# Naturals at three quarters of the prior unit, row stores and bias additions later, warm-up transposes, gate and up in one stage

## The chip, the cores and the metric

The kernel runs on one core of one Trainium2 chip. The metric is device time in microseconds (us) of one execution, as the median of a few runs. A profile is one more execution, taken by the hardware profiler. TensorE is called PE, VectorE DVE, ScalarE ACT, GpSimd POOL, and SP (SyncE) only issues DMAs.

## What is computed

x is (2, 1024, 256) in float32, 2048 rows of 256. Its layer norm xn feeds a causal attention with 16 heads of 16 and a mixture of 8 experts with the two best per row; both are added to x.

```
xn = layernorm(x)
q, k, v = xn @ Wq + bq, xn @ Wk + bk, xn @ Wv + bv        # 16 heads of 16
attn = softmax(q @ k.T * 0.25 + causal) @ v, heads joined, @ Wo + bo
logits = xn @ Wr; the two largest, softmax over the two
moe = sum over the two: p * ((clip(silu(xn @ Wg[e]), -7, 7) * (xn @ Wu[e])) @ Wd[e])
out = x + attn + moe
```

## The kernel before

**Shapes and tiles.** The 2048 rows are 16 tiles of 128. Heads are taken four at a time, so attention is 8 units (UNITS: two batches by four groups). A unit has 12 steps (STEPS), each of one block of 128 keys against up to 512 queries, for four heads. In a step the scores are transposed (keys on partitions), the exponential is taken by ACT from PSUM (`exps`, line 838), POOL masks the diagonal blocks (`mask`, line 776), and PE weighs v (`weigh_v`, line 1232) into one bank per 512 queries.

**Naturals and negated maxima.** The exponential needs the row maximum first. So each unit's scores are also computed the natural way round (`natural`, line 1194, queries on partitions, 48 chunks a unit), DVE takes the maximum of each (`row_max`, lines 939 and 942), negates them and splits them into three bfloat16 parts (lines 956 to 959), PE transposes them (line 1200), DVE copies them to negt (line 966), and SP copies negt by DMA into three extra rows of packq (`neg_rows`, line 665). The first scores of the unit (`scores`, line 1213) wait for that copy. The naturals of unit u run beside the scores of unit u - 1.

**q and k.** PE projects them (`qk_product`, line 1125), ACT takes the high part in bfloat16 (line 810), DVE the residual (line 911), ACT the middle part (line 816), POOL the low part (line 738). SP stores all parts to DRAM (line 642) and loads them packed by head for each unit (`load`, line 655: three runs, each for q and for k, for each half: twelve DMAs a unit). There are three slots (SLOTS), so the loads of unit u wait for the last scores of unit u - 3.

**Start.** SP loads x in four parts, DVE takes mean and variance and writes xn (line 902) into the memory that probs uses later, PE transposes it (`transpose_xn`, line 1118), ACT copies it, and ACT's queue stores xn to DRAM (`store_xn`, line 795) for the gathers. The first exponential and the first gather wait for these stores. v and the router's logits come from line 1149.

**Experts.** After routing (DVE, lines 1004 to 1090, and PE lines 1157 to 1175) 39 tiles of 128 rows are worked on: POOL gathers rows (line 752) and fetches the expert's weights (line 762, 3 slots) by indirect DMA, PE transposes the rows (line 1265), does gate and up as two stages `gu1` and `gu2` into one bank (line 1272), ACT takes tanh (line 866), DVE makes the hidden values (lines 1097, 1100), PE multiplies down (line 1293), ACT scales (line 872), POOL scatters the rows to DRAM (line 768). POOL also adds the output bias to x, tile by tile (`add_bias_to_x`, line 744); the attention projection (line 1258) is added to that later (line 998), and SP reads the expert rows back and DVE adds them (lines 987, 989).

**Order.** At build time a planner (`Planner`, `make_plan`) lists all stages as jobs with an engine, a cost in ns, what they come after, a due time, a lag until the result is seen, the PSUM bank they take or free, and a size for large DMAs (bytes over 65536 count at 280 per ns on one common line). It goes through them greedily: for each engine the job that can start first, ties by due time (on PE, 8000 is added to the due of a kind other than the one before), and of the engines the earliest. The result is a fixed list per engine and the bank of each result; each engine then walks its list (`walk`) and waits on semaphores. The planner's numbers only set the order; they are not waits. Attention is due from 40000 to 415000 ns, the experts from 85000 to 375000. These lines set what the change touches:

```
return begin + (end - begin) * 0.9 * sum(nat_weight[:m]) / sum(nat_weight)      # nat_due, line 260
job("ACT", ("ln", q), 420, [("DVE", ("ln", q))], due=2000 + q, lag=2000, size=524288)      # row stores, line 271
job("POOL", ("residual", t), 700, [("DVE", ("bias",)), ("DVE", ("ln", 3))], 110000 + 8000 * t)      # line 319
```

## Time and profile before

| | us |
|---|---|
| runs, median of 3 | 490.92 |
| runs, lowest and highest | 488.54, 501.08 |
| profiled execution, its own time | 493.95 |
| its span in the profile | 492.1 |

Start times are microseconds from the start of the span; the span is shorter than the execution's own time by what lies around it. A row of the timeline or of a group names the engine (PEld is PE's weight load, SPq the queue that SP issues into), the line, the operation, out<-in and the count; in brackets stands how long the engine was idle before it and what ended that. PEclk is the granted TensorE clock as a share of full speed. In this profile a matmul of float32 is recorded as two.

### The profile page before, as it was taken

Reading aid. Unit: us, or ns where it says so; the run is one execution under the profiler, and the core shown is the slowest. Engines: PE = TensorE matmul, PEld = TensorE weight load, DVE = VectorE, ACT = ScalarE, POOL = GpSimd, SP = SyncE. Lnnn points to the kernel's source line nnn. Section 1 sums busy time; section 2 is a strip of 40 time slices with the busy share of each in tenths; the row PEclk is TensorE's granted clock in tenths of the full one; section 3 lists DMA queues with packets and bytes.
Section 4 is the critical chain, followed back from the end, with each engine's and each line's share of the span. In section 5 each row is a group of like instructions: output and inputs, shape, how many; then the busy total and the mean of one; then the engine's idle time right before and its main releaser. Section 6 shows DMA issues by size and latency. Waiting matters only on the chain.

```text
span 492.1 us, 8376 instructions
## 1 busy us (share of the span) xinstructions
PE 433.8 (88%) x2791; PEld 255.0 (52%) x2791; DVE 323.1 (66%) x1007; ACT 245.0 (50%) x607; POOL 200.3 (41%) x239
## 2 busy tenths in 40 slices
PE   0995973968997999899979999799979999999996
PEld 0673531553234456465655666456646565566443
DVE  4824899669786577656646558456665675766394
ACT  0561562231564564565436444565465545664972
POOL 4320289553025126343535246334454365433211
PEclk9997996887898999899989999999999999999999
DMA  8379861481009226943594229624394454340491
GB/s 269 133 215 160 170 143 65 142 285 44 1 20 224 113 77 194 185 133 117 188 199 159 85 98 230 148 84 168 113 252 130 153 161 128 128 156 15 151 313 52
DMA packets 40374, 71.35 MB, mean 145 GB/s; under 512 B 5893, under 2 KB 30598, under 8 KB 40332
## 3 DMA queue, kind: packets, MB, share of 16 engines
q0 software_dynamic: 9360, 39.99, 25.5%
q1 hardware_dynamic: 27996, 27.54, 24.2%
q10 hardware_dynamic: 2976, 3.29, 2.1%
q8 instruction: 23, 0.38, 0.3%
q14 instruction: 19, 0.16, 0.1%
HBM read 55.85 MB, written 15.60 MB: 145 GB/s over the span
## 4 chain that ended last, share of the span: by engine, by line
PE 48%; issue 23%; DVE 9%; DMA 8%; ACT 5%; POOL 4%; SPq 3%; POOLq 0%; ACTq 0%; DVEq 0%
PE psum L1232 9%; PE psum L1213 9%; PE psum L1272 9%; PE psum L1194 9%; PE psum L1293 5%; ACT probs L838 3%; DMA packq<-negt 3%; SPq L655 2%; DVE psum L939 2%; PE psum L1125 2%; DMA x<-in_x 2%; DMA packk<-qk_parts 2%; PE psum L1258 2%; POOL probs L776 1%; DMA xg<-xn_rows,token 1%
## 5 line engine op out<-in xcount | busy, mean ns | idle before, releaser
L838 ACT ACTIVATE probs<-psum 128x512 f32<-128x512 f32 (+3 forms) x384 | 159.4, 507 | 74.7 <-PE psum L1213 65.4
L939 DVE CUSTOM_DVE_ANT_0 psum<-psum,maskrow 128x128 f32<-128x128 f32 (+3 forms) x256 | 122.2, 504 | 45.2 <-PE psum L1194 44.6
L1213 PE MATMUL psum<-packq,packk 99*128 99x512 bf16 (+3 forms) x384 | 99.7, 343 | 16.3 <-DMA packq<-negt 11.3
L1194 PE MATMUL psum<-packk,packq 96*128 96x512 bf16 (+3 forms) x384 | 100.8, 344 | 7.8 <-DMA packk<-qk_parts 5.5
L942 DVE TENSOR_REDUCE mxa<-psum 128x1 f32<-128x512 f32 x128 | 87.8, 686 | 20.1 <-PE psum L1194 19.8
L1232 PE MATMUL psum<-probs,v 128*32 128x512 f32 (+3 forms) x768 | 79.1, 505 | 9.6 <-POOL probs L776 8.7
L1272 PE MATMUL psum<-xgt,wexp 128*128 128x128 f32 x624 | 84.6, 282 | 0.2 <-ACT xgt L859 0.2
L1272 PEld LDWEIGHTS psum<-xgt,wexp 128*128 128x128 f32 x624 | 80.2, 197 | 8.5 <-issue 6.0
L776 POOL TENSOR_SCALAR_AFFINE_SELECT probs<-probs 128x512 f32<-128x512 f32 x64 | 43.9, 689 | 96.8 <-ACT probs L838 96.2
L762 POOL DMA_INDIRECT wexp<-in_wexp,wrow x39 | 37.5, 960 | 93.8 <-PE psum L1293 87.0
L1213 PEld LDWEIGHTS psum<-packq,packk 99*128 99x128 bf16 x384 | 34.9, 99 | 70.8 <-issue 21.7
L1194 PEld LDWEIGHTS psum<-packk,packq 96*128 96x128 bf16 x384 | 36.7, 100 | 51.4 <-issue 12.5
L752 POOL DMA_INDIRECT xg<-xn_rows,token x39 | 37.8, 968 | 26.8 <-PE psum L1265 20.1
L768 POOL DMA_INDIRECT expert_rows<-yo,slots x39 | 39.9, 1023 | 17.0 <-issue 11.1
L1293 PE MATMUL psum<-wexp,hid 128*128 128x256 f32 x156 | 42.6, 396 | 0.5 <-ACT probs L838 0.3
L1097 DVE SCALAR_TENSOR_TENSOR tanh<-tanh,psum 128x256 f32<-128x256 f32 x39 | 16.3, 418 | 35.2 <-ACT tanh L866 31.4
L1232 PEld LDWEIGHTS psum<-probs,v 128*32 128x32 f32 x768 | 18.1, 110 | 36.2 <-issue 26.5
L1293 PEld LDWEIGHTS psum<-wexp,hid 128*128 128x128 f32 x156 | 26.8, 191 | 18.5 <-issue 11.1
L872 ACT ACTIVATE yo<-psum 128x256 f32<-128x256 f32 x39 | 15.0, 385 | 42.5 <-PE psum L1293 42.0
L738 POOL TENSOR_TENSOR stage<-resid,stage 128x512 bf16<-128x512 f32 x16 | 19.8, 1246 | 36.9 <-ACT stage L816 36.8
L1125 PE MATMUL psum<-xnt,wqk 128*128 128x512 f32 x64 | 33.3, 634 | 1.0 <-DVE prod L1037 1.0
L866 ACT ACTIVATE tanh<-psum 128x256 f32<-128x256 f32 x39 | 15.1, 388 | 31.3 <-PE psum L1272 30.7
(114 smaller groups left out, 385.9 us busy)
## 6 DMA issues: line engine op xcount, KB each, us to landing
qk_parts<-stage SPq DMA_DIRECT2D x24, 256.0 KB, 3.2
stage<-expert_rows SPq DMA_DIRECT2D x16, 256.0 KB, 4.3
packq<-qk_parts SPq DMA_DIRECT2D x16, 192.0 KB, 5.4
packk<-qk_parts SPq DMA_DIRECT2D x16, 192.0 KB, 5.7
x<-in_x SPq DMA_DIRECT2D x4, 512.0 KB, 9.2
xn_rows<-probs ACTq DMA_DIRECT2D x4, 512.0 KB, 3.2
packq<-qk_parts SPq DMA_DIRECT2D x16, 128.0 KB, 6.1
packk<-qk_parts SPq DMA_DIRECT2D x16, 128.0 KB, 5.9
```

Of the source, the lines that this page charges most:

```text
L752: pool.indirect_dma_start(out=xg[:, i % 2, :], out_offset=None, in_=xn_d, in_offset=bass.IndirectOffsetOnAxis(ap=token[:, i:i + 1], axis=0))\
L768: pool.indirect_dma_start(out=z_d, out_offset=bass.IndirectOffsetOnAxis(ap=slots[:, i:i + 1], axis=0), in_=yo[:, i % 2, :], in_offset=None ...
L776: pool.affine_select(out=cols, in_=cols, compare_op=ALU.is_ge, fill=0.0, base=0, pattern=[[0, UH], [1, P]], channel_multiplier=-1).then_in ...
L838: act.activation(probs[:, g % RING, h, 0:width], psum[:, bank, 0:width], ACT.Exp, scale=SCALE)\
L939: ins = dve.tensor_tensor_reduce(out=chunk, in0=chunk, in1=maskrow[:, BANK - width:], scale=1.0, scalar=NEG, op0=ALU.add, op1=ALU.max, acc ...
L942: ins = dve.tensor_reduce(into, chunk, op=ALU.max, axis=AX.X)
L1125: return pe.matmul(psum[:, bank, :], wqk[:, op, c, P * grp:P * (grp + 1)], xnt_moe[:, c, cols], start=c == 0, stop=c == DC - 1)
L1194: pe.matmul(psum[:, bank, 0:width], packq[0:MAXROW, u % SLOTS, i // HALF, h, P * (i % HALF):P * (i % HALF + 1)], packk[0:MAXROW, u % SLOTS ...
L1213: pe.matmul(psum[:, bank, 0:width], packk[0:KROWS, u % SLOTS, j // HALF, h, P * (j % HALF):P * (j % HALF + 1)], packq[0:KROWS, u % SLOTS, ...
L1232: ins = pe.matmul(psum[32 * h:32 * h + 32, bank, t0 - BANK * c:BANK], v[:, TB * b + j, at:at + 32], probs[:, g % RING, h, 0:width], start= ...
L1272: ins = pe.matmul(psum[:, bank, P * m:P * (m + 1)], wexp[:, i % WSLOTS, at:at + P], xgt[:, i % 2, c, :], start=c == 0, stop=c == DC - 1)
L1293: ins = pe.matmul(psum[:, bank, 0:D], hid[:, i % 2, P * c:P * (c + 1)], wexp[:, i % WSLOTS, at:at + D], start=c == 0, stop=c == DC - 1)
```

## The change

- `nat_due`: the naturals of a unit are due over the first 0.75 (SPREAD) of the prior unit and not 0.9.
- The lag of the copy of the negated maxima (`("SP", ("neg", x))`) is 8000 (NEG_LAG) and not 2200.
- The row stores of xn (`("ACT", ("ln", q))`) are due at 34000 and not 2000, and come after the first load of unit 0.
- The bias addition of tile t (`("POOL", ("residual", t))`) comes after scatter t in POOL's list.
- The loads of unit 1 are due at 60000 and not 20000; the loads of unit 0 have a lag of 4500 and not 2500.
- Gather, fetch and scatter cost 1250, 1300 and 1300 and not 1000; a gather counts with 131072 bytes and has a lag of 2200.
- `gu1` and `gu2` become one stage `gu` of 1850, in `gate_up`: the same products in the same order, with nothing between them.
- Before its list PE does 60 (WARM) transposes of the identity into bank 7, as soon as the first constants are there.

No wait on a semaphore is added or taken away other than the one in `warm_clock`; the lists of all engines are planned anew.

```diff
--- before.py
+++ after.py
@@ -234,8 +234,11 @@
 SWITCH = {("b", "b"): 5, ("f", "f"): 15, ("b", "f"): 95, ("f", "b"): 20, ("b", "c"): 105, ("f", "c"): 105,
           ("c", "b"): 110, ("c", "f"): 120}
 STAY = 8000
+NEG_LAG = 8000
+SPREAD = 0.75
 RATE = 280
 SMALL = 65536
+WARM = 60
 PACE = dict(attention=(40000, 415000), experts=(85000, 375000))
 
 
@@ -257,7 +260,7 @@
         if u == 0:
             return 5000 if m < EARLY else 30000 + 400 * (m - EARLY)
         begin, end = due_at[NS * (u - 1)], due_at[NS * u]
-        return begin + (end - begin) * 0.9 * sum(nat_weight[:m]) / sum(nat_weight)
+        return begin + (end - begin) * SPREAD * sum(nat_weight[:m]) / sum(nat_weight)
 
     for n, (ns, due) in enumerate(((1100, -30), (2000, 30), (1800, 31))):
         job("POOL", ("const", n), ns, due=due)
@@ -268,7 +271,7 @@
         job("DVE", ("stats", q), 1900, [("SP", ("x", q))], due=10 * q)
         job("POOL", ("rstd", q), 960, [("DVE", ("stats", q))], due=-20)
         job("DVE", ("ln", q), 1280, [("POOL", ("rstd", q))], due=10 * q - 5)
-        job("ACT", ("ln", q), 420, [("DVE", ("ln", q))], due=2000 + q, lag=2000, size=524288)
+        job("ACT", ("ln", q), 420, [("DVE", ("ln", q)), ("SP", ("load", 0, 0, 0))], due=34000 + q, lag=2000, size=524288)
         for c in range(DC):
             pe(("xnt", q, c), 436, [("DVE", ("ln", q))], due=10 * q, takes=("xnt", q, c))
             job("ACT", ("xnt", q, c), 478, [("PE", ("xnt", q, c))], due=10 * q, frees=("xnt", q, c))
@@ -316,7 +319,7 @@
     pe(("bias",), 853, [("DVE", ("widen",))], 30000, takes=("bias",))
     dve(("bias",), 425, [("PE", ("bias",))], 30000, frees=("bias",))
     for t in range(NT):
-        job("POOL", ("residual", t), 700, [("DVE", ("bias",)), ("DVE", ("ln", 3))], 110000 + 8000 * t)
+        job("POOL", ("residual", t), 700, [("DVE", ("bias",)), ("DVE", ("ln", 3)), ("POOL", ("scatter", t))], 110000 + 8000 * t)
 
     for u in range(UNITS):
         b, g = divmod(u, G)
@@ -324,9 +327,9 @@
             after = [("SP", ("store", 4 * b + 2 * (g // 2) + c))]
             if u >= SLOTS:
                 after += [("PE", ("s", NS * (u - SLOTS + 1) - 1, UH - 1))]
-            due = 8 + 10 * c if u == 0 else 20000 + c if u == 1 else nat_due(u, 0) - 30000 + c
+            due = 8 + 10 * c if u == 0 else 60000 + c if u == 1 else nat_due(u, 0) - 30000 + c
             for r in range(len(RUNS)):
-                job("SP", ("load", u, c, r), 900, after, due, lag=2500, size=131072)
+                job("SP", ("load", u, c, r), 900, after, due, lag=2500 if u else 4500, size=131072)
 
     for u in range(UNITS):
         for m in range(NCH):
@@ -340,7 +343,7 @@
         dve(("negate", x), 1200, [("DVE", ("max", u, m))], due)
         pe(("neg", x), 60, [("DVE", ("negate", x))], due, ("neg", x), "b")
         dve(("neg", x), 220, [("PE", ("neg", x))], due, ("neg", x))
-        job("SP", ("neg", x), 550 if c1 - c0 == 2 else 1600, [("DVE", ("neg", x))], 0, lag=2200, size=8192)
+        job("SP", ("neg", x), 550 if c1 - c0 == 2 else 1600, [("DVE", ("neg", x))], 0, lag=NEG_LAG, size=8192)
 
     for g in range(NS * UNITS):
         u, n = divmod(g, NS)
@@ -387,20 +390,19 @@
         after = [("DVE", ("list",)), ("ACT", ("ln", 3))] if i == 0 else []
         if i >= 2:
             after += [("PE", ("x", i - 2))]
-        job("POOL", ("gather", i), 1000, after, due - 8000, lag=2000)
+        job("POOL", ("gather", i), 1250, after, due - 8000, lag=2200, size=131072)
         after = [("DVE", ("experts",)), ("PE", ("list",))] + ([("PE", ("d", i - WSLOTS))] if i >= WSLOTS else [])
-        job("POOL", ("fetch", i), 1000, after, due - 9000, lag=2000, size=128 * WROW * 4)
+        job("POOL", ("fetch", i), 1300, after, due - 9000, lag=2000, size=128 * WROW * 4)
         pe(("x", i), 220, [("POOL", ("gather", i))], due, ("x", i))
-        job("ACT", ("xgt", i), 252, [("PE", ("x", i))] + ([("PE", ("gu2", i - 2))] if i >= 2 else []), due,
+        job("ACT", ("xgt", i), 252, [("PE", ("x", i))] + ([("PE", ("gu", i - 2))] if i >= 2 else []), due,
             frees=("x", i))
-        pe(("gu1", i), 875, [("ACT", ("xgt", i)), ("POOL", ("fetch", i))], due + 500, ("gu", i))
-        pe(("gu2", i), 875, [("PE", ("gu1", i))], due + 500)
-        job("ACT", ("tanh", i), 280, [("PE", ("gu2", i))] + ([("DVE", ("hid", i - 2))] if i >= 2 else []), due + 1000)
+        pe(("gu", i), 1850, [("ACT", ("xgt", i)), ("POOL", ("fetch", i))], due + 500, ("gu", i))
+        job("ACT", ("tanh", i), 280, [("PE", ("gu", i))] + ([("DVE", ("hid", i - 2))] if i >= 2 else []), due + 1000)
         dve(("hid", i), 780, [("ACT", ("tanh", i))] + ([("PE", ("d", i - 2))] if i >= 2 else []), due + 1000, ("gu", i))
         pe(("d", i), 853, [("DVE", ("hid", i))], due + 2000, ("d", i))
         job("ACT", ("yo", i), 280, [("PE", ("d", i))] + ([("POOL", ("scatter", i - 2))] if i >= 2 else []), due + 2000,
             frees=("d", i))
-        job("POOL", ("scatter", i), 1000, [("ACT", ("yo", i))], due + 2000, lag=1800)
+        job("POOL", ("scatter", i), 1300, [("ACT", ("yo", i))], due + 2000, lag=1800)
 
     for t in range(NT):
         after = [("POOL", ("scatter", MAX_TILES - 1)), ("SP", ("store", QKS // 2 - 1)), ("DVE", ("gates",))]
@@ -415,7 +417,7 @@
 
 
 ORDER, BANK_OF, PLANNED = make_plan()
-FIRST_OF = {"qk1": "qk", "gu1": "gu"}
+FIRST_OF = {"qk1": "qk"}
 
 
 def fill_of(stage):
@@ -1109,6 +1111,11 @@
 
         @block.tensor
         def _(pe):
+            def warm_clock():
+                pe.wait_ge(consts, 1)
+                for _ in range(WARM):
+                    pe.transpose(psum[:, BANKS - 1, 0:P], ident[:, :], ident[:, :])
+
             def transpose_xn(q, c):
                 if q == 0 and c == 0:
                     pe.wait_ge(consts, 1)
@@ -1265,25 +1272,16 @@
                     ins = pe.transpose(psum[:, bank, P * c:P * (c + 1)], xg[:, i % 2, P * c:P * (c + 1)], ident[:, :])
                 ins.then_inc(full, 1)
 
-            def gu_product(i, m):
-                bank, _ = FILL_AT[("gu", i)]
-                for c in range(DC):
-                    at = 2 * F * c + P * m
-                    ins = pe.matmul(psum[:, bank, P * m:P * (m + 1)], wexp[:, i % WSLOTS, at:at + P], xgt[:, i % 2, c, :],
-                                    start=c == 0, stop=c == DC - 1)
-                return ins
-
-            def gate_up_first(i):
+            def gate_up(i):
                 pe.wait_ge(fetch_in[i % WSLOTS], 16 * (i // WSLOTS + 1))
                 wait_freed(pe, ("x", i))
-                wait_room(pe, ("gu", i))
-                for m in range(F // P):
-                    gu_product(i, m)
-
-            def gate_up(i):
-                for m in range(F // P, 2 * F // P):
-                    ins = gu_product(i, m)
-                ins.then_inc(filled[FILL_AT[("gu", i)][0]], 1)
+                bank, full = wait_room(pe, ("gu", i))
+                for m in range(2 * F // P):
+                    for c in range(DC):
+                        at = 2 * F * c + P * m
+                        ins = pe.matmul(psum[:, bank, P * m:P * (m + 1)], wexp[:, i % WSLOTS, at:at + P], xgt[:, i % 2, c, :],
+                                        start=c == 0, stop=c == DC - 1)
+                ins.then_inc(full, 1)
 
             def down(i):
                 wait_freed(pe, ("gu", i))
@@ -1294,10 +1292,11 @@
                                     start=c == 0, stop=c == DC - 1)
                 ins.then_inc(full, 1)
 
+            warm_clock()
             walk("PE", {"xnt": transpose_xn, "qk1": project_qk_first, "qk2": project_qk, "v": project_v, "route": route,
                         "list": list_tokens, "bias": project_bias, "nat": natural, "neg": transpose_neg, "s": scores,
                         "pv": weigh_v, "y_t": transpose_y, "proj_t": transpose_heads, "proj": project, "x": transpose_rows,
-                        "gu1": gate_up_first, "gu2": gate_up, "d": down})
+                        "gu": gate_up, "d": down})
 
 
 _SHAPES = {
```

## Rows read from the trace of the kernel before

**Rows 1.** The page, part 1: busy time, share of the span, instructions

```profile
PE 433.8 (88%) x2791; PEld 255.0 (52%) x2791; DVE 323.1 (66%) x1007; ACT 245.0 (50%) x607; POOL 200.3 (41%) x239
```

**Rows 2.** Windows by stage; the first row names the columns

```profile
core 0: us, PE busy (x) PEld busy (x) DVE busy (x) ACT busy (x) POOL busy (x), PEclk, DMA share, GB/s
...
42.35:64.00 21.65, 21.65 (x104) 13.03 (x105) 17.61 (x99) 8.53 (x22) 5.19 (x5) 0.92 0.94 167
64.00:86.00 22.00, 11.68 (x57) 3.61 (x56) 21.48 (x30) 9.12 (x22) 19.76 (x21) 0.79 0.38 96
86.00:148.00 62.00, 54.77 (x285) 25.90 (x284) 49.41 (x159) 22.92 (x50) 20.39 (x22) 0.85 0.30 99
148.00:460.00 312.00, 295.60 (x2080) 182.50 (x2079) 195.62 (x619) 169.82 (x428) 135.71 (x156) 0.98 0.51 143
```

**Rows 3.** What PE waited for: total us, times, longest us

```profile
PE psum L1213 <- DMA packq<-negt: 11.3, 5, 3.2
PE psum L1232 <- POOL probs L776: 8.7, 8, 5.1
...
PE psum L1213 <- issue: 2.6, 2, 1.9
```

**Rows 4.** Timeline at the starts of two units: start us, us, what

```profile
243.67 0.30 SPq L655 DMA_DIRECT2D packq<-qk_parts  x1
...
246.41 0.73 SPq L665 DMA_DIRECT2D packq<-negt  x1
...
253.69 1.43 PE L1213 MATMUL psum<-packq,packk 99*128 99x512 bf16 x4 [3.21 <-DMA packq<-negt]
...
452.23 0.71 SPq L665 DMA_DIRECT2D packq<-negt  x1
...
455.32 1.04 PE L1213 MATMUL psum<-packq,packk 99*128 99x512 bf16 x4 [0.66 <-DMA packq<-negt]
```

**Rows 5.** Windows, a stretch after a hole

```profile
156.00:160.00 4.00, 4.00 (x16) 1.58 (x15) 3.03 (x12) 3.60 (x11) 1.31 (x3) 0.50 1.08 255
```

**Rows 6.** The page, part 5: groups by line

```profile
L939 DVE CUSTOM_DVE_ANT_0 psum<-psum,maskrow 128x128 f32<-128x128 f32 (+3 forms) x256 | 122.2, 504 | 45.2 <-PE psum L1194 44.6
...
L942 DVE TENSOR_REDUCE mxa<-psum 128x1 f32<-128x512 f32 x128 | 87.8, 686 | 20.1 <-PE psum L1194 19.8
...
L1272 PEld LDWEIGHTS psum<-xgt,wexp 128*128 128x128 f32 x624 | 80.2, 197 | 8.5 <-issue 6.0
...
L768 POOL DMA_INDIRECT expert_rows<-yo,slots x39 | 39.9, 1023 | 17.0 <-issue 11.1
```

**Rows 7.** Timeline, PE at the start

```profile
12.82 3.65 PE L1118 MATMUL psum<-ident,probs 128*128 128x128 f32 x16 [12.82 <-DVE probs L902]
...
16.26 4.81 PE L1125 MATMUL psum<-xnt,wqk 128*128 128x512 f32 x8
...
21.79 3.60 PE L1125 MATMUL psum<-xnt,wqk 128*128 128x512 f32 x8
...
25.23 1.91 PE L1118 MATMUL psum<-ident,probs 128*128 128x128 f32 x16
```

**Rows 8.** Timeline, up to the first natural

```profile
26.00 1.27 ACT L810 ACTIVATE stage<-psum,bqk 128x512 bf16<-128x512 f32 x2 [2.48 <-DVE probs L902]
...
32.10 0.48 SPq L655 DMA_DIRECT2D packq<-qk_parts  x1
...
42.35 0.82 PE L1194 MATMUL psum<-packk,packq 96*128 96x128 bf16 x3 [5.48 <-DMA packk<-qk_parts]
```

**Rows 9.** Bias additions by their line; the timeline of a mask

```profile
L744 POOL TENSOR_TENSOR x<-x,bo x16: 717/730/1286, 62.3 to 85.4; 128x256 f32<-128x256 f32 x16
...
76.49 2.69 POOL L776 TENSOR_SCALAR_AFFINE_SELECT probs<-probs 128x512 f32<-128x512 f32 x1
...
79.32 1.51 PE L1232 MATMUL psum<-probs,v 128*32 128x384 f32 x8 [5.07 <-POOL probs L776]
```

**Rows 10.** Timeline, the transposes of the second gather

```profile
103.05 0.44 PE L1265 MATMUL psum<-ident,xg 128*128 128x128 f32 x2 [3.85 <-DMA xg<-xn_rows,token]
```

## The prediction

> **What bounds the kernel now.** I read the busy times of the engines first. PE is busy 433.8 of 492.1 us, DVE 323.1, ACT 245.0, POOL 200.3 [rows 1]. So PE bounds it, and the time can fall in two ways: PE stands still for less than its 58.3 us, or its busy time shrinks because less of it runs at the lower of the clock's two levels (1.2 instead of 2.4 GHz). The windows by stage [rows 2] say where both lie. Standing still (length less busy): 10.3 us at 64 to 86, 7.2 at 86 to 148, 16.4 at 148 to 460. Lost to the clock ((1 - PEclk) x busy): 1.7 us at 42 to 64, 2.5 at 64 to 86, 8.2 at 86 to 148, 5.9 at 148 to 460. Then the list of what PE waited for: the copy of the negated maxima into packq 11.3 us, masked probability tiles 8.7, "issue" ahead of a score 2.6 [rows 3]; and single rows for 12.82 us before the first transpose [rows 7], 5.48 before the first natural [rows 8], 3.85 for a gather [rows 10]. The change aims at all of these but the 12.82.
>
> Every engine walks a fixed list that the planner wrote. At each step it takes the job that can start soonest, and a due time decides only among jobs that can start at the same instant. So a later due does not hold a job back on an idle engine; a dependency, a longer lag or a longer cost does.
>
> **The naturals and the lag of the negated maxima.** Take the stretch around 250. The loads that an old unit's end sets free begin at 243.67; the copy of the maxima is issued at 246.41, six loads ahead of it and six behind; PE stands from 250.48 to 253.69 [rows 4]. That is 7.3 us from issue to use. The copy at 452.23, with no loads beside it, had its scores at 455.32, 3.1 us later, with 0.66 us of standing [rows 4]. The plan reckoned 2.2 us. With SPREAD 0.75 the naturals end earlier by 0.15 of a unit's pace of (415 - 40) / 8 = 46.9 us, that is 7.0 us; so the copy would go out near 239.4, ahead of the loads, and land near 242.5. With NEG_LAG 8 us the plan puts other stages between besides. What can go is 11.3 + 2.6 = 13.9 us [rows 3]. The loads themselves remain, with fetches and gathers beside them, so some wait returns under another name. I take -10 (from -13.9 to -3).
>
> After such a hole PE comes back at the low level: at 156 to 160 the granted clock is 0.50 with PE busy for all 4 us [rows 5]. The 5.9 us of clock at 148 to 460 are of this kind: -4.5 (-5.9 to 0).
>
> The price is a denser DVE. From 148 to 460 it is busy 195.6 of 312 us, 63% [rows 2]. Its maxima take (87.8 + 122.2) / 323.1 = 65% of its busy time [rows 1, 6], so 0.41 of the time. In the stretch where naturals lie that makes 0.41 / 0.9 + 0.22 = 68% now and 0.41 / 0.75 + 0.22 = 77% then. It has room, but on PE a natural whose bank isn't free stops everything behind it. One reduction takes 0.686 us [rows 6]; half a one waited for in every third of the 7 x 12 steps that have naturals beside them is 9.6 us, none is 0. No wait for maxima is among PE's large ones now, so I take a third: +3 (0 to +10).
>
> **The start.** PE begins at 12.82. Its first 16 transposes take 3.65 us against 1.91 for 16 later ones, and its first 8 records of L1125 4.81 against 3.60 [rows 7]. So it starts at the low level: the 8 records are 1.21 us too long, which is 2.4 us at half pace, so the rise came near 18.7. Sixty transposes from the ready identity on (near 1.9) run at 3.44 / 16 = 0.215 us each, start to start, at the low level and 0.119 at the high one. If the clock rises 4 to 5.6 us in, they are through near 11, in time that is idle anyway, and the two groups run 1.7 + 1.2 = 2.9 us shorter. If it never rises, they end at 14.8, 2.0 us late.
> The row stores move behind the first load in ACT's list. The fourth now waits for the last rows, and the high parts of the next two tiles stand behind it: they start at 26.00, after 2.48 us of ACT idle [rows 8]. They can go some 1.5 us earlier; residual, middle and low part, store and first load (32.10) follow. Against this, 2 MB of row stores now flow beside the loads, which need from 32.10 to 42.35 as it is [rows 8]. At the 255 GB/s of window 156 to 160 [rows 5], 2 MB are 8.2 us of all queues; between none and half of it falls ahead of the first natural, I take 1. The later due of unit 1's loads does nothing: SP is idle and takes them at once. So -2.9 - 1.5 + 1, about -3.5 (-6 to +3). The first exp comes after 64, so the stores have time to land.
> On the clock a page speaks against the sixty transposes. What this trace shows: the rise near 18.7 came 5.9 us after the first transpose but 2.4 us after the first product of L1125 [rows 7]; from 42.35 on, with PE busy throughout, a mean of 0.92 over 21.65 us is 3.5 us at the low level [rows 2]. The Trainium skill ("TensorE: Matmul & The Clock Gate", Part 4) says that transposes do not count as busy for the clock. By that rule the warm-up costs the 2.0 us and the sum is 4.9 us higher; this trace leans the other way, products alone having needed 3.5 us and not 2.4.
>
> **Bias additions.** Their due of 110 us did nothing: all 16 lie between 62.3 and 85.4, 0.73 us in the median and up to 1.29 [rows 9], among the masks. The mask of 76.49 took 2.69 us, and PE stood 5.07 us for it [rows 9]. Tied to scatters, which come far behind the routing, they leave POOL free and this mask starts up to 2 us sooner; how long it takes beside the DVE stays open. 8.7 us of mask waits are there in all [rows 3]; they bound it. But until 86 the DVE's routing (busy 21.48 of 22 us [rows 2]) decides what follows. PE's product of the token list stands behind the waits, so experts can begin earlier. -3 (-8.7 to 0). The 16 x 0.73 us come back among gathers, on a POOL that is 43% busy.
>
> **Costs of gather, fetch, scatter.** A scatter measured 1.02 us with 11.1 / 39 = 0.28 of issue ahead of it [rows 6]; the plan had 1.0 and gets 1.3. PE stood 3.85 us for the second gather at 103.05 [rows 10]; now the plan counts its bytes and can put naturals there. -2 (-4 to +2). With an earlier start and fewer holes up to 148, some of the 12.4 us of clock before 148 returns, but there the DVE sets the pace: -2 (-6 to +2).
>
> **Gate and up in one stage.** No product goes. The weight loads of L1272 have 8.5 us of idle before them, 6.0 by "issue" [rows 6], mostly where another kind stood between the halves. I take a quarter; and a score may now wait up to half a stage more: -1.5 (-3 to +1).
>
> **Sum.** -10 - 4.5 + 3 - 3.5 - 3 - 2 - 2 - 1.5 = -23.5 on the profiled execution's own 493.95 us (span 492.1 and 1.85 around it): 470.5. The median of the runs shown is 490.92, 0.6% less; 470.5 x 490.92 / 493.95 = 467.6, so 468.
>
> **Rivals.**
> (1) *The hole is the load burst, not the maxima.* If full queues hold up fetches, gathers and instructions as well, the row of the maxima vanishes and its time returns under other names: the -14.5 shrink to -3, 482 on the profile, 479. For it: 2.6 us go by "issue", with no engine named [rows 3], and DMA share is 1.08 beside the low clock [rows 5]. Against: PE's row names the copy, and the copy free of loads cost 0.66 us.
> (2) *The start gives nothing.* The clock does not rise and the row stores delay the first load: +2 in place of -3.5 gives 476, so 473. For it the loads' 10 us as they are; against, the dated rise.
> (3) *The early stretch gives more.* The token list and the experts move up by the whole wait, and half of the 12.4 us of clock comes back: 9 us more, 461.5, so 459. Against: the DVE's 21.48 of 22 us.
> (4) *Slower: the DVE becomes the bound.* Naturals pressed into three quarters make PE wait a whole reduction, 0.686 us, at each step. Without the +3 the gains are 26.5 us; 39 such waits undo them and 53 make it slower by 2%. There are 84 steps; at 60 it is 41 us: 508.6, so 505. For it: PE's fixed order; against: 77%.
>
> **How the numbers follow.** Forecast 0.60, (1) 0.15, (2) 0.13, (3) 0.08, (4) 0.04. The forecast's own terms, taken as independent, give about 11 us to each side. The range reaches below (3) and above (1): 455 to 484. Two per cent, about what a measurement of this kernel can tell from no change, is 481. Below it lie the forecast, (2), (3) and over half of (1), less tails: 0.84 faster, 0.12 within, 0.04 slower.
>
> **What would show it.** Right: under 3 us of waits for the copy; SP issues the copy ahead of a unit's loads; the first records of L1125 at 0.45 us each; no bias addition before 120; first natural near 39; PE idle under 9 us at 148 to 460; granted clock over 0.97. Wrong: a new wait for wexp or xg of 10 us; scores or naturals waiting over 10 us for maxima; PE busy, warm-up left out, not under 428.

## The result and the profile after

The changed kernel takes 464.67 us in the median of four runs (459.69 to 469.68), the kernel before 492.27 (488.54 to 501.08): a ratio of 0.939 (0.926 to 0.953). All ratios of this document are taken from the fast executions of each kernel alone, so they are not the quotients of the medians beside them. A second series gave 474.01 against 498.82, 0.955 (0.949 to 0.961). Forecast were 468 us and a range of 455 to 484. The profiled execution is the slowest of its four, 469.68 us with a mean granted clock of 0.960; the fastest, 459.69, had 0.985, and the fastest of the second series, 471.72, had 0.967.

Page of the changed kernel, part 1, against [rows 1]:

```profile
PE 436.3 (93%) x2851; PEld 261.7 (56%) x2851; DVE 317.2 (68%) x1007; ACT 242.3 (52%) x607; POOL 197.9 (42%) x239
```

Sixty more PE instructions and 24.2 us less of span (467.9 for 492.1). The windows say where, against [rows 2] (PE stands for a window's length less its busy time):

```profile
core 0: us, PE busy (x) PEld busy (x) DVE busy (x) ACT busy (x) POOL busy (x), PEclk, DMA share, GB/s
0.00:86.00 86.00, 73.78 (x374) 44.39 (x375) 62.46 (x212) 35.70 (x88) 33.92 (x48) 0.94 0.68 187
86.00:148.00 62.00, 54.06 (x301) 31.92 (x301) 51.47 (x172) 22.63 (x53) 21.32 (x24) 0.86 0.41 125
148.00:440.00 292.00, 286.76 (x2046) 173.25 (x2047) 187.85 (x589) 170.63 (x434) 139.94 (x164) 0.99 0.52 148
440.00:468.00 28.00, 21.67 (x133) 12.15 (x130) 15.41 (x36) 13.32 (x34) 2.71 (x4) 0.94 0.48 155
```

The same windows of the kernel before:

```profile
0.00:86.00 86.00, 57.38 (x251) 33.47 (x252) 58.01 (x188) 33.26 (x83) 39.48 (x56) 0.91 0.70 165
...
148.00:440.00 292.00, 276.46 (x1934) 170.46 (x1933) 184.30 (x585) 156.66 (x393) 128.34 (x146) 0.98 0.54 150
```

PE stands still for 5.2 us at 148 to 440 where it had stood for 15.5. Up to 86 it stands for 12.2 instead of 28.6, but 8.1 of these 16.4 us are filled by the warm-up. From 86 to 148 it stands 7.9, against 7.2 [rows 2]. So the standing time falls by 26.7 us in all (58.3 to 31.6); the warm-up takes 8.1 back, and the busy time without it falls by 5.6 (433.8 to 428.2): 26.7 - 8.1 + 5.6 = 24.2.

What PE waited for, against [rows 3]:

```profile
engine line waited for: us in total, times, longest us
PE psum L1282 <- DMA wexp<-in_wexp,wrow: 5.6, 2, 3.9
PE psum L1125 <- DVE probs L904: 2.7, 2, 2.4
PE psum L1201 <- DVE prod L1039: 2.4, 1, 2.4
...
PE psum L1239 <- POOL probs L778: 1.8, 4, 0.7
```

The copy of the maxima (11.3 us before) has no row left, the masks fell from 8.7 to 1.8. At the start of a unit the copy now leaves ahead of all twelve loads, here by 4.8 us, and the scores that need it (231.20, 8.6 us after its issue) run without a wait, where [rows 4] had six loads ahead of it and 3.21 us of standing:

```profile
222.63 0.73 SPq L667 DMA_DIRECT2D packq<-negt  x1
227.40 0.31 SPq L657 DMA_DIRECT2D packq<-qk_parts  x1
...
231.20 1.03 PE L1220 MATMUL psum<-packq,packk 99*128 99x512 bf16 x4
```

One large hole beside a burst is left, in another unit: weights are fetched at 145.20, at the end of twelve loads issued from 138.81 to 145.27, and PE waits for them until 150.06. (The other 1.8 us of this row, at 117.12, have no loads beside them.)

```profile
145.20 0.98 POOL L764 DMA_INDIRECT wexp<-in_wexp,wrow  x1 [0.30 <-PE psum L1272]
...
150.06 3.78 PE L1282 MATMUL psum<-xgt,wexp 128*128 128x128 f32 x16 [3.85 <-DMA wexp<-in_wexp,wrow]
```

After it the 16 products take 3.78 us, against 2.0 for such a stage elsewhere (101.10), and the granted clock of 150 to 154 is 0.50: the low level behind a hole is seen again.

The start, against [rows 7, 8]:

```profile
2.01 8.14 PE L1117 MATMUL psum<-ident 128*128 128x128 f32 x60 [2.01 <-POOLq L729]
...
12.57 1.07 PE L1125 MATMUL psum<-ident,probs 128*128 128x128 f32 x8 [2.43 <-DVE probs L904]
...
14.87 3.60 PE L1132 MATMUL psum<-xnt,wqk 128*128 128x512 f32 x8
...
28.67 0.49 SPq L657 DMA_DIRECT2D packq<-qk_parts  x1
...
36.74 0.76 PE L1201 MATMUL psum<-packk,packq 96*128 96x128 bf16 x5
```

The 60 transposes are through at 10.15. The next eight take 1.07 us, 0.134 each, in spite of 2.43 us of idle between; the first records of the q and k product take 3.60, not 4.81. The first load comes 3.4 us earlier, the first natural 5.6. The row stores went out at 35 to 37 as meant. The bias additions moved too (62.3 to 85.4 before [rows 9]), though not behind 120 as the prediction had it:

```profile
L746 POOL TENSOR_TENSOR x<-x,bo x16: 723/740/771, 104.2 to 255.0; 128x256 f32<-128x256 f32 x16
```

Yet a faster start shows little at the end, as the runs below say.

### The profile page after: what moved, and what is told of

Its sections match the earlier page's. It is cut to its first block, busy times and chain, and to the rows that moved or that the text cites. A ratio compares the mean times of both kernels' runs of the same rounds, so it can differ in the third digit from the quotient of the medians.

```text
span 467.9 us, 8496 instructions
## 1 busy us (share of the span) xinstructions
PE 436.3 (93%) x2851; PEld 261.7 (56%) x2851; DVE 317.2 (68%) x1007; ACT 242.3 (52%) x607; POOL 197.9 (42%) x239
## 4 chain that ended last, share of the span: by engine, by line
PE 72%; DMA 12%; DVE 5%; ACT 4%; issue 3%; POOL 2%; SPq 1%; ACTq 0%; POOLq 0%
PE psum L1282 15%; PE psum L1239 14%; PE psum L1220 13%; PE psum L1201 11%; PE psum L1291 7%; DMA xg<-xn_rows,token 4%; PE psum L1265 3%; DMA qk_parts<-stage 3%; DMA wexp<-in_wexp,wrow 3%; ACT probs L840 3%; PE psum L1132 2%; PE psum L1156 2%; DMA x<-in_x 2%; PE psum L1272 2%; PE psum L1247 1%
## 5 line engine op out<-in xcount | busy, mean ns | idle before, releaser
L840 ACT ACTIVATE probs<-psum 128x512 f32<-128x512 f32 (+3 forms) x384 | 156.1, 515 | 39.4 <-PE psum L1220 38.8
L944 DVE TENSOR_REDUCE mxa<-psum 128x1 f32<-128x512 f32 x128 | 88.0, 687 | 28.7 <-PE psum L1201 28.7
L1201 PE MATMUL psum<-packk,packq 96*128 96x512 bf16 (+3 forms) x384 | 97.5, 333 | 3.8 <-DVE prod L1039 2.4
L1220 PE MATMUL psum<-packq,packk 99*128 99x512 bf16 (+3 forms) x384 | 98.0, 335 | 2.8 <-DVE mxa L944 1.2
L1239 PE MATMUL psum<-probs,v 128*32 128x512 f32 (+3 forms) x768 | 78.0, 507 | 2.8 <-POOL probs L778 1.8
L770 POOL DMA_INDIRECT expert_rows<-yo,slots x39 | 39.6, 1015 | 23.2 <-ACT yo L874 12.3
L874 ACT ACTIVATE yo<-psum 128x256 f32<-128x256 f32 x39 | 15.0, 385 | 42.3 <-PE psum L1291 36.7
L740 POOL TENSOR_TENSOR stage<-resid,stage 128x512 bf16<-128x512 f32 x16 | 18.4, 1164 | 32.5 <-ACT stage L818 32.5
L1132 PE MATMUL psum<-xnt,wqk 128*128 128x512 f32 x64 | 30.7, 600 | 0.8 <-DVE resid L913 0.8
```

What stands on the lines that cost most here:

```text
L770: pool.indirect_dma_start(out=z_d, out_offset=bass.IndirectOffsetOnAxis(ap=slots[:, i:i + 1], axis=0), in_=yo[:, i % 2, :], in_offset=None ...
L840: act.activation(probs[:, g % RING, h, 0:width], psum[:, bank, 0:width], ACT.Exp, scale=SCALE)\
L944: ins = dve.tensor_reduce(into, chunk, op=ALU.max, axis=AX.X)
L1132: return pe.matmul(psum[:, bank, :], wqk[:, op, c, P * grp:P * (grp + 1)], xnt_moe[:, c, cols], start=c == 0, stop=c == DC - 1)
L1201: pe.matmul(psum[:, bank, 0:width], packq[0:MAXROW, u % SLOTS, i // HALF, h, P * (i % HALF):P * (i % HALF + 1)], packk[0:MAXROW, u % SLOTS ...
L1220: pe.matmul(psum[:, bank, 0:width], packk[0:KROWS, u % SLOTS, j // HALF, h, P * (j % HALF):P * (j % HALF + 1)], packq[0:KROWS, u % SLOTS, ...
```

## The experiments

Three series, each on one chip with runs of the kernel before beside it; ratios are to that. The first has the changed kernel again, no warm-up, the row stores early and the naturals back; the second the copy first, the two constants alone, the long lag without the early naturals and the bias additions free; the third all others. Only the first has the changed kernel in it. That kernel came out at 0.939 (the result above) and 0.955, so a ratio of one series is compared with one of another to no better than 1.6%, some 8 us.

### The changed kernel again, and three of its parts undone

The changed kernel:

> The changed kernel itself, for comparison on the same chip. Ratio to the kernel before 0.94 (0.93 to 0.95). If its runs differ by over 1% among themselves again, the differences should follow the granted clock (0.96 to 0.985 so far), not the waits.

474.01 us, 0.955 (0.949 to 0.961).

Without the warm-up:

```diff
-WARM = 60
+WARM = 0
```

> The changed kernel with WARM 0; all lists stay as they are. Theory A, the start is on the path: the first 16 transposes and the first 8 records of L1132 run at the low level, 2.9 us more, first natural at 39 to 40 instead of 36.7, the whole 3 us slower than the changed kernel. Theory B, the DVE's routing swallows it: first natural as late, but the token list's product at about the same time (76) and the whole within 1 us. Theory C, transposes do not count for the clock: nothing changes in the first groups.

472.67 us, 0.949 (0.941 to 0.956): no slower. The first natural is at 38.6 instead of 36.7, but the token list at 74.9 against 75.4. Its first transposes:

```profile
12.96 3.38 PE L1125 MATMUL psum<-ident,probs 128*128 128x128 f32 x16 [12.96 <-DVE probs L904]
16.18 3.60 PE L1132 MATMUL psum<-xnt,wqk 128*128 128x512 f32 x8
```

Here the q and k product begins 1.3 us later than in the changed kernel and runs at the high level from its first record. So the clock came up during 16 transposes, with only idle time before them. In the kernel before the same 16 had not brought it up by their end, and the product behind them took 4.81 us [rows 7]; of the four kernels traced here without a warm-up two rose by the end of the 16 and two behind it. The Trainium skill ("TensorE: Matmul & The Clock Gate", Part 4) says that a transpose does not count as busy for the clock in the way of other products. These two rows, and the 1.07 us behind the sixty, speak against that for float32 transposes as this kernel does them.

The row stores ahead of the first load again:

```diff
-        job("ACT", ("ln", q), 420, [("DVE", ("ln", q)), ("SP", ("load", 0, 0, 0))], due=34000 + q, lag=2000, size=524288)
+        job("ACT", ("ln", q), 420, [("DVE", ("ln", q))], due=2000 + q, lag=2000, size=524288)
```

> The changed kernel with the row stores due at 2000 and without their dependency, as before; only ACT's list changes. Theory A, the fourth store's wait holds up the high parts: first load 1.5 to 2 us later than 28.67 and the whole 1 to 2 us slower. Theory B, stores beside loads cost more than the wait: first load later, but the loads land faster, so that the first natural comes no later than 36.7 and the whole is the same or up to 1 us faster.

473.45 us, 0.952 (0.947 to 0.957). The first load goes out at 30.9, not 28.7, and the first natural at 38.7, not 36.7; the end does not move. Not all of the 2 us are the stores': in this trace PE was idle for 2.03 us behind the 60 transposes, the granted clock was 0.50 from 13 to 16, the 16 transposes of xn took 3.49 us, and the first product began at 16.10, not 14.87. So the warm-up did not hold the level in this execution.

The naturals and the lag as before, the rest of the change kept:

```diff
-NEG_LAG = 8000
-SPREAD = 0.75
+NEG_LAG = 2200
+SPREAD = 0.9
```

> The changed kernel with SPREAD 0.9 and NEG_LAG 2200. Theory A, the copy of the maxima makes the holes: its waits come back (over 8 us in the list of PE's waits), with 4 us of clock, and the whole is 12 to 15 us slower than the changed kernel, ratio to before 0.965 to 0.97. Theory B, the load burst makes them: the row of the copy comes back, the waits for wexp (5.6 us) go, the whole is 3 to 5 us slower, ratio 0.945 to 0.95.

485.73 us, 0.976 (0.969 to 0.982), 11.7 us above the changed kernel on the same chip. What PE waited for:

```profile
PE psum L1220 <- DMA packq<-negt: 15.5, 6, 4.0
```

The wait is back, longer than in the kernel before. The two constants are worth 11.7 us here, and all the rest of the change together 13.1 (498.82 to 485.73).

### Is it the copy's place in the queue?

The two constants do two things: they move naturals, and they change the plan's order on SP, where every copy now stands ahead of later units' loads. The kernel before had two, one, three and five of the plan's loads (each is two DMAs) of later units ahead of the copies of units 1 to 4. The next kernel is the kernel before with that order alone changed, everything else as planned:

```diff
+for _x in range(2, len(NEGS)):
+    _sp = ORDER["SP"]
+    _at = _from = _sp.index(("neg", _x))
+    while _sp[_from - 1][0] == "load" and _sp[_from - 1][1] > _x:
+        _from -= 1
+    _sp[_from:_at + 1] = [_sp[_at], *_sp[_from:_at]]
```

> The kernel before; only SP's list changes: each copy of the negated maxima from unit 1 on goes ahead of the loads of later units that stood just before it. All other lists stay. Theory A, the copy waits for the loads issued ahead of it: it lands about 3 us after issue instead of 7, PE's waits for it fall from 11.3 to under 4 us, and with some clock the whole is 6 to 10 us faster than before, ratio 0.98 to 0.985. Theory B, the loads behind it hold it up as much as those ahead of it: waits stay over 8 us, ratio 0.995 to 1.0. Theory C, the burst moves on to other waits: the copy's row falls, others for wexp or xg rise by as much, ratio 0.995 to 1.0.

481.93 us against 492.88, 0.974 (0.968 to 0.981). Its windows and its wait at the same unit start as in [rows 4]:

```profile
148.00:440.00 292.00, 284.72 (x1998) 177.13 (x1996) 190.16 (x605) 162.47 (x407) 131.30 (x150) 0.98 0.55 154
```

```profile
236.85 0.73 SPq L671 DMA_DIRECT2D packq<-negt  x1
237.69 0.39 SPq L661 DMA_DIRECT2D packq<-qk_parts  x1
...
243.69 1.89 PE L1219 MATMUL psum<-packq,packk 99*128 99x512 bf16 x4 [2.43 <-DMA packq<-negt]
```

Standing time at 148 to 440 falls from 15.5 to 7.3 us, and the waits for the copy from 11.3 to 5.9. The copy goes out 9.6 us earlier, yet with twelve loads right behind it still takes 6.8 us from issue to use (7.3 in [rows 4], 3.1 with no loads near). The kernel before had one copy ahead of its burst too, and PE waited 2.71 us for it:

```profile
354.92 0.73 SPq L665 DMA_DIRECT2D packq<-negt  x1
...
361.62 1.04 PE L1213 MATMUL psum<-packq,packk 99*128 99x512 bf16 x4 [2.71 <-DMA packq<-negt]
```

There it is 5.3 us with two load DMAs ahead (194.31 to 199.62), 7.3 with six, 9.9 with ten (302.96 to 312.84), and 6.7 with none. So for most copies the place in the queue buys an earlier issue more than a quicker landing; being first does not give the 3.1 us. Whether it is the loads behind it that slow it was not separated: a fetch of expert weights (768 KB) goes out up to 1 us before the copies at 236.85 and 354.92 too, and none beside the one that took 3.1. Moving 22 load DMAs behind four copies is worth some 11 us with no instruction more or less.

The two constants alone, on the kernel before:

```diff
-        job("SP", ("neg", x), 550 if c1 - c0 == 2 else 1600, [("DVE", ("neg", x))], 0, lag=2200, size=8192)
+        job("SP", ("neg", x), 550 if c1 - c0 == 2 else 1600, [("DVE", ("neg", x))], 0, lag=NEG_LAG, size=8192)
```

(and 0.75 for 0.9 in `nat_due`, NEG_LAG = 8000)

> The kernel before with SPREAD 0.75 and NEG_LAG 8000 alone. Theory A, this part is worth 11.5 us by itself (-10 of waits, -4.5 of clock, +3 of denser DVE): ratio 0.975 to 0.98. Theory B, the parts need each other: the first 150 us stay as they are, and the later gain is under 5 us, ratio over 0.99. The copy's row goes to under 1 us in either.

489.87 us, 0.997 (0.993 to 1.001). The plan has every copy ahead of later units' loads here as well. No wait for the copy is left in its list; others are there:

```profile
PE psum L1234 <- POOL probs L778: 11.3, 10, 5.1
PE psum L1196 <- ACT yo L874: 5.3, 1, 5.3
```

The span is 488.8, the standing time 54.5 us against 58.3. It lies elsewhere now: a natural waits 5.28 us at 157.87 for a bank that ACT's `yo` was to free, masks cost 2.6 us more, and the end after 440 has 9.5 us of standing instead of 6.9. So the copy wait can be removed and nothing gained, if the new plan has holes of its own.

The long lag kept, the naturals at 0.9 again, in the changed kernel:

```diff
-SPREAD = 0.75
+SPREAD = 0.9
```

> The changed kernel with SPREAD 0.9 and NEG_LAG 8000 kept. Theory A, the lag alone makes the plan put other stages before the scores: waits for the copy stay under 3 us although it goes out beside the loads, and the whole is within 4 us of the changed kernel. Theory B, the early issue is what counts: waits for the copy over 5 us, 8 us slower or more.

482.59 us, 0.979 (0.974 to 0.984). Its list of waits, and one unit start:

```profile
PE psum L1272 <- DMA xg<-xn_rows,token: 14.1, 4, 5.9
PE psum L1282 <- DMA wexp<-in_wexp,wrow: 4.6, 2, 3.0
```

```profile
227.94 0.73 SPq L667 DMA_DIRECT2D packq<-negt  x1
...
229.50 0.95 POOL L754 DMA_INDIRECT xg<-xn_rows,token  x1 [0.30 <-issue]
...
238.63 0.69 PE L1272 MATMUL psum<-ident,xg 128*128 128x128 f32 x2 [5.85 <-DMA xg<-xn_rows,token]
```

The copy is issued behind eight of the twelve loads again. The plan allows it 8 us and puts expert work in the gap; but that work's gather was issued in the same burst, and PE waits for it until 238.63, 9.1 us after its issue. Of the copy a wait of 1.9 us is left in all. This is rival (1), the hole under another name; in this kernel it holds as long as the copy stays in the burst.

Last, both constants undone in the changed kernel (as in the 485.73 us kernel above), with the copies moved ahead by the six lines:

> The changed kernel with SPREAD 0.9 and NEG_LAG 2200 (which cost 2.1% of the time before, 0.9756 against 0.9551), but with each copy of the maxima put ahead of the loads of later units in SP's list. Theory A, the order on SP's queue is all that the naturals part brings: ratio 0.95 to 0.96, PE's waits for the copy fall from 15.5 us to under 6. Theory B, the copy's head start of some 7 us is needed too: waits for it stay at 6 to 9 us and the ratio at 0.96 to 0.97.

468.79 us against 501.06, 0.943 (0.937 to 0.948).

```profile
PE psum L1226 <- DMA packq<-negt: 3.8, 2, 3.2
```

The order alone brings back what the constants brought, within what two series can tell: with naturals at 0.9 and a lag of 2.2 us, 0.976 without the order becomes 0.943 with it. Two kernels of the same series that keep the constants, with one other part undone each, took 463.80 and 464.39 us, so up to 5 us may be theirs.

### The bias additions

```diff
-        job("POOL", ("residual", t), 700, [("DVE", ("bias",)), ("DVE", ("ln", 3)), ("POOL", ("scatter", t))], 110000 + 8000 * t)
+        job("POOL", ("residual", t), 700, [("DVE", ("bias",)), ("DVE", ("ln", 3))], 110000 + 8000 * t)
```

> The changed kernel with the bias additions free to start on an idle POOL, as before; POOL's list changes, PE's in a twelfth of its places. Theory A, they hold up masks and so the token list: its product comes 3 to 5 us later than 75.9, and the whole is 3 us slower than the changed kernel. Theory B, DVE alone sets the early stretch: the product stays within 1 us of 75.9 and the whole within 1 us.

468.40 us against 492.88, 0.952 (0.947 to 0.957). They run at 57.2 to 79.0 again, and the token list comes at 79.9 instead of 75.4. Whether these 4 us reach the end stays open: 0.952 lies between the changed kernel's 0.955 and 0.939 of two other series, and a loss of 3 us is less than that can show.

### The plan's costs, the lag of the loads, and the halves of gate and up

Costs of gather, fetch and scatter at 1000, the gather with a lag of 2000 and without its bytes:

> The changed kernel with gather, fetch and scatter at 1000 and a gather without bytes. Theory A, the real costs keep PE from meeting gathers and scatters before they land: waits for xg, wexp and what stands behind scatters rise from 6 us to over 12, whole 5 to 8 us slower. Theory B, they matter little: within 2 us.

464.39 us against 501.06, 0.934 (0.928 to 0.941).

```profile
86.00:148.00 62.00, 58.85 (x374) 36.82 (x374) 54.49 (x184) 26.44 (x64) 32.37 (x37) 0.94 0.61 179
```

PE stands 3.2 us in this stretch instead of 7.9, at a clock of 0.94 instead of 0.86. The truer costs bought nothing there.

The lag of unit 0's loads at 2500:

> The changed kernel with unit 0's loads at a lag of 2500 again. Theory A, the longer lag lets the v products be done while the loads fly, so that routing starts early: without it DVE's first routing instruction comes 3 us or more later than 46.9, the token list's product at 79 or later, and PE is idle for 5 us more at 64 to 88; whole 3 to 5 us slower. Theory B, the early stretch has no path to the end: the product comes later, the whole stays within 2 us, as with the bias additions.

463.80 us, 0.932 (0.927 to 0.937): no loss either. Both are at or a little below the changed kernel's 0.939 and 0.955; as they were not timed beside it, that either is faster stays open.

Gate and up as two stages again, with the functions for them as in the kernel before:

```diff
-        pe(("gu", i), 1850, [("ACT", ("xgt", i)), ("POOL", ("fetch", i))], due + 500, ("gu", i))
+        pe(("gu1", i), 875, [("ACT", ("xgt", i)), ("POOL", ("fetch", i))], due + 500, ("gu", i))
+        pe(("gu2", i), 875, [("PE", ("gu1", i))], due + 500)
```

> The changed kernel with gate and up as two stages again. Forecast of the prediction: 1.5 us slower. Rival from the busy times: PE's busy time less its clock loss is 415.2 us before and 415.0 after without the warm-up, so the merged stage saved nothing and the whole stays within 1 us.

484.21 us against 501.06, 0.971 (0.963 to 0.979). In the same series the three kernels with one stage, each with another part undone, took 463.80, 464.39 and 468.79: 15 to 20 us less. Against the changed kernel, in other series, it is 0.971 / 0.955 to 0.971 / 0.939, 1.7 to 3.4%: 8 to 16 us. Its windows:

```profile
86.00:148.00 62.00, 53.13 (x271) 25.76 (x271) 50.23 (x170) 20.00 (x48) 17.80 (x21) 0.82 0.41 117
148.00:440.00 292.00, 282.10 (x1963) 174.77 (x1962) 183.96 (x582) 159.93 (x404) 136.93 (x160) 0.98 0.49 142
440.00:486.00 46.00, 36.46 (x251) 20.20 (x249) 21.46 (x50) 26.08 (x69) 8.76 (x12) 0.96 0.42 138
```

Up to 86 it does the same as the changed kernel. By 440 it has 251 matmuls left where the other has 133. Of the 18.2 us between the two profiled spans (486.1 and 467.9) 8.2 are standing time and 10.0 more busy time, about 5 of these by the clock ((1 - PEclk) x busy is 21 us in all against 16). The first expert tile shows how this starts. With one stage, in the changed kernel:

```profile
87.60 3.75 PE L1282 MATMUL psum<-xgt,wexp 128*128 128x128 f32 x16 [1.27 <-issue]
...
95.06 0.42 DVE L1099 SCALAR_TENSOR_TENSOR tanh<-tanh,psum 128x256 f32<-128x256 f32 x1
...
98.01 1.08 PE L1291 MATMUL psum<-wexp,hid 128*128 128x256 f32 x4
```

With two:

```profile
88.14 1.66 PE L1280 MATMUL psum<-xgt,wexp 128*128 128x128 f32 x8 [0.51 <-issue]
...
90.14 2.00 PE L1280 MATMUL psum<-xgt,wexp 128*128 128x128 f32 x8
...
134.52 1.99 PE L1301 MATMUL psum<-wexp,hid 128*128 128x256 f32 x8
```

With two stages the down product of the first tile comes at 134.52 (147.57 in the kernel before), and the first scatter at 137.2 (150.2). With one it comes at 98.01, the scatter at 100.6. Up to 148 there are 80 records of gate and up products and 20 of down products in the changed kernel, 56 and 12 with two stages. The halves are no slower themselves, 1.05 to 1.13 us each at the high level against 2.0 for both. What comes after them is late. DVE's first hidden values, with two stages:

```profile
113.76 0.41 DVE L1100 SCALAR_TENSOR_TENSOR tanh<-tanh,psum 128x256 f32<-128x256 f32 x1
114.20 0.42 DVE L1103 SCALAR_TENSOR_TENSOR hid<-tanh,psum 128x256 f32<-128x256 f32 x1
```

ACT's tanh for them was done at 92.6, so they stood 21 us in DVE's list, and another 20 in PE's until 134.52. In the changed kernel the same step begins at 95.06, 3.3 us after its tanh. Why the plan puts them so late when the stage is halved was not settled. In every kernel run here with one stage the first scatter lies at 97 to 103, in every one with two at 137 to 151. That halving the stage costs the time is shown; that it costs it by the late down products is read from these rows and was not tested by itself.

## Why the prediction was right, and where it was not

The total, 468 against 464.67, is nearer than the steps deserve.

**Naturals, copy and clock behind the holes.** Forecast -10 and -4.5, with +3 against them: -11.5. Undoing the two constants costs 11.7 us; doing only what they do to SP's order gains 11 on the kernel before. The mechanism was the one named: the copy went out behind the loads. That it takes naturals ending 7.0 us earlier to put it right was half of it: the order does it without them. And that the two constants are worth this by themselves was wrong: on the kernel before, with the order they bring and no wait for the copy left, they gave 0.997. Nor does a copy ahead of the loads land in the 3.1 us that the prediction gave it (near 242.5 for 239.4): it took 6.8. What helped is that it went out earlier, by 9.6 us with the order alone.

**Denser DVE, +3.** Hardly seen. The waits for maxima come to 1.2 and 0.3 us at most in the changed kernel, those for the negated maxima to 2.3 (0.7 before). Rival (4) falls with it.

**Start, -3.5; bias additions, -3; early clock, -2.** On the spot they came, and larger: the first natural 5.6 us earlier, the token list at 75.9 instead of 88.2, mask waits 8.7 to 1.8. At the end, the warm-up and the row stores taken back alone gave no loss (0.949 and 0.952 beside 0.955 in their series); for the bias additions it can't be told (0.952 beside 0.939 and 0.955 of others). So the step that failed is "experts can begin earlier", taken as a gain at the end: for the start no run shows one. Of the warm-up the prediction had that the 60 are "through near 11", with a rise 4 to 5.6 us in, for which it gave no row; in ten traces they took 8.07 to 9.62 us from 2.0 on, and in nine of these the level held to the transposes of xn. The 0.119 us that it gives for a transpose at the high level, start to start, is 1.91 / 16, with the last one's tail; the next product of that trace starts at 26.97, so start to start it is (26.97 - 25.23) / 16 = 0.109. That changes nothing in the sum. In the profile PE still stands 7.9 us between 86 and 148, and the clock lost there and before is 12.3 us against 12.4 ((1 - PEclk) x busy for 42 to 148: 0.5 + 4.2 + 7.6). For the start this is what rival (2) forecast for the end, by another way than it named: the clock did rise and the load was not delayed. All of them undone together was not tried.

**Costs and lags, -2.** No gain is seen, perhaps a slight loss: 0.934 and 0.932 without them, beside 0.939 and 0.955 of other series. The later due of unit 1's loads was taken as without effect and is: with 20000 the plan writes the same lists for all engines.

**Gate and up in one stage, -1.5.** The term that was mis-sized. It was priced by idle time ahead of weight loads (8.5 us [rows 6]), which is where halves lie apart. It measured 8 to 16 us, and, as far as the rows show, by another path: the plan gets its first down product 36 us earlier (98 against 134). That the row of down products in the trace of before stood 44 us behind the first gate and up product (103.32 to 147.57) was there to be read, and was not.

So two things carry the change: the copy ahead of the loads, 11 us, and one stage for gate and up, 8 to 16; together 19 to 27, against 22 to 30 measured (0.955 and 0.939). That they add up is reckoned, not shown: no kernel had these two alone, and that the parts act on each other is seen at the two constants, which gave 11.7 us with the others and 0.3% without. The forecast had -1.5 for the second and -10.5 for start, bias, costs and early clock, 12 in all: about what the one stage alone measured. That the total came out is luck. Rival (1) was right as to what a burst does, and wrong that the copy could not be taken out of it. Rival (3), 459, named the early stretch; the run median lies between it and the forecast.

**The signs.** Right: no copy row; the copy ahead of the loads; L1132 at 0.45 us a record; first natural before 39; standing time at 148 to 460 8.9 us, just under 9. Not met: bias additions from 104, not 120. Of the signs of being wrong, one came by a hair: PE busy without warm-up is 428.2, not under 428, in this execution. The clock of 0.97 was met in the faster runs and missed in the profiled one (0.96).

## What to carry to other kernels

Where a small DMA that releases a critical stage shares a queue with a burst of large loads, look first at its place in the queue: six lines that reorder it gave 2.6% with nothing else changed, and a longer lag in the plan without that order moved the wait to the next DMA in the burst. Being first did not make the copy quick (6.7 and 6.8 us); what helped is that it went out earlier. In a kernel with a planned order, an edit that takes no work away, such as one stage for two, can be worth as much as those that shorten waits; here it came with a long chain that starts earlier. Search the trace for the first time that the last link of a chain runs. And waits removed early in the kernel are worth nothing until an experiment shows them at the end.

## What was not expected of the hardware

- A copy of this kind takes 6.7 and 6.8 us from issue to use even when it is the first of its burst, 5.3 as the third, 7.3 as the seventh, 9.9 as the eleventh and 3.1 alone.
- During sixteen float32 transposes after 13 us of idle PE came to the high level in two traces of four, and not by their end in the two others. After sixty of them the level held over 2.43 us of idle in the changed kernel, and over 1.3 to 2.5 in eight others, but fell to 0.50 after 2.03 us in the one with the row stores early.
- Four executions of one kernel ran from 459.69 to 469.68 us with the mean granted clock from 0.985 to 0.960, and the kernel before from 493.2 (0.955) to 502.37 (0.932) on one chip. Differences of one profile under 2% say little here.
